# Edge sum of a graph layer: three of a group's seven edge lists get no blocks, their source rows are gathered edge by edge

## The chip, the cores and the metric

The kernel runs on one core of a Trainium2 chip. Its time is the device time of one execution in microseconds (us). TensorE is called PE in the profile (PEld is its weight loads), VectorE is DVE, ScalarE is ACT, GpSimd is POOL, and SyncE, which only issues transfers here, is SP.

## The reference, cut to what matters

```python
# x: 6250 x 256; src, dst: 200000 edges, sorted by dst; edge_weight: 200000
xn = _layernorm(x)
# _L0_gnn_ref: row = src, col = dst
gathered = edge_weight[:, None] * xn[dst]
gnn = segment_sum(gathered, src, 6250) + node_vec1
x = x + gnn + mix(xn)                 # linear attention, 4 heads
x = x + experts(_layernorm(x))        # 8 experts, the best 2 of each row
```

All is float32. The change lies in the second and third line: each edge adds its weight times row `dst` of `xn` to row `src` of the sum.

## The kernel before, in words

The 6250 rows are held as 49 tiles of 128 rows. `front` normalizes the rows and writes them to `xn_dram`; `edge_sum` makes the sum over the edges; `stragglers` looks for edges that found no place (none here); `route` and `experts` do the rest.

`edge_sum` has two jobs that run beside each other.

**Sorting.** Since the edges are sorted by `dst`, the edges of one dst tile lie in a row, and 49 steps `s` take one dst tile each. A step puts its edges into 49 lists by src tile, 128 slots a list (a list of one dst tile and one src tile is called a cell here). It needs `base` on PE (34 matmuls, L767), `hot_tiles`, `in_row`, `rank`, `slots` and `values` on VectorE (L992 to L1029) and `make_table` on PE (34 matmuls, L776). Its result, for each slot the src row in its tile, the dst row in its tile and the weight as three bfloat16 parts (FIELDS = 5), is copied by ScalarE into `table`. Eight steps run ahead of the sum (`schedule`, `sort`); the other 41 are spread over the sum's steps.

**Summing.** Seven dst tiles make a group `g` (7 groups), and for each group the kernel goes over the 49 src tiles: 343 steps `t`. Seven steps are a unit (`unit`, 49 units in all); the 42 units of the first six groups carry a sorting step each, the 7 units of the last group carry the normalization of the finished rows instead. A step `t` does, for the cells j = 0 to 6 of its group:

- VectorE, `hots` (L1063, L1067): one-hot matrices of the src and of the dst rows, slots on the partitions (`hots`, 2 x 7 x 128 elements a partition), and the src ones times the three parts of the weight (`hot_w`, 3 x 7 x 128).
- PE, `blocks` (L803): 7 x 3 bfloat16 matmuls, which sum over the slots and give for each cell a block, dst row by src row, of weights, in PSUM.
- ScalarE, `evacuate` (L910, L911): the seven blocks to `block_sb`.
- PE, `rows` (L811): 7 float32 matmuls, block times the 128 rows of the dst tile in `window`, summed in PSUM.
- VectorE, `add` (L1085): the sum to `acc`.

Each engine runs its instructions in the order in which `unit` writes them, and waits on semaphores. `blocks` of step t + 1 stand ahead of `rows` of step t; `hots` runs two steps ahead, `add` one behind. `cur` holds a unit's table values, each repeated 16 times by ScalarE (`take`, L904). GpSimd has no work in `edge_sum`. It issues transfers with row numbers from on-chip memory (indirect DMAs) only in `experts`: two gathers of 128 rows of 1032 bytes from `z_dram` (L1643) and two scattering additions into `sum_dram` (L1652) for each of 56 pieces.

## Time and profile before

| | us |
|---|---|
| median of 3 runs | 2680.07 |
| lowest, highest | 2675.88, 2681.29 |
| profiled execution | 2681.12 |
| its span | 2679.3 |

| stage (from, to in the span) | us | what runs |
|---|---|---|
| 0 to 415 | 415 | `front`, and eight sorting steps ahead |
| 415 to 1932 | 1517 | units 0 to 41: sum with sorting beside it |
| 1932 to 2168 | 236 | units 42 to 48: sum with normalization |
| 2168 to 2679 | 511 | `route`, `experts` |

The trace lists each instruction with its start and length; equal ones in a row are merged, and their length is that of the whole run. A float32 matmul has two records, so 7 matmuls of `rows` stand as x14. The waits that are printed name what an idle engine waited for; "issue" is time in which the engine waited for nothing that the profile shows.

### The profile page before, as it was taken

To read this page: it belongs to the slowest core of one execution; us is meant where nothing else is said; L and a number is where in the kernel's file an instruction comes from. 1 tells how busy PE (TensorE), PEld (TensorE's weight loads), DVE (VectorE), ACT (ScalarE), POOL (GpSimd) and SP (SyncE) were. 2 spreads that over 40 slices of the span, in tenths; PEclk is the share of its full clock that TensorE was granted. 3 is DMA by queue.
4 is the path that set the end of the run, shared out by engine and by line. 5 is a ranking of instruction groups with operands and counts; after the bars stand their busy time and mean duration, and the time that the engine had idled before them with its cause. 6 is when DMAs were issued, how large, how long until landed. Compare 5 with 4: busy or idle time off the path is not lost. (4 is left out here: it accounts for less than half of the span.)

```text
span 2679.3 us, 52157 instructions
## 1 busy us (share of the span) xinstructions
PE 2339.9 (87%) x19629; PEld 2059.4 (77%) x19630; DVE 2149.8 (80%) x2716; ACT 1382.2 (52%) x1876; POOL 451.9 (17%) x335
## 2 busy tenths in 40 slices
PE   4884679999999999999999999999999944999994
PEld 2553557888888888888888888888889944989983
DVE  5775769888988888898888899888888866766663
ACT  1223556556565555655555565555533324666662
POOL 2562000000000000000000000000000023888883
PEclk8997779999999999999999999999999967999997
DMA  6322230000000000000000000000011152444455
GB/s 159 85 81 80 69 97 15 0 0 2 14 0 0 15 1 0 0 15 1 0 0 16 1 0 0 15 0 0 1 42 56 56 168 45 75 76 76 75 78 129
DMA packets 124275, 103.46 MB, mean 39 GB/s; under 512 B 44684, under 2 KB 117879, under 8 KB 123892
## 3 DMA queue, kind: packets, MB, share of 16 engines
q1 hardware_dynamic: 95920, 71.42, 9.0%
q0 software_dynamic: 21504, 29.49, 7.2%
q10 hardware_dynamic: 6724, 0.83, 0.3%
q8 instruction: 83, 1.36, 0.2%
q14 instruction: 44, 0.36, 0.1%
HBM read 54.60 MB, written 53.51 MB: 40 GB/s over the span
## 5 line engine op out<-in xcount | busy, mean ns | idle before, releaser
L811 PE MATMUL bank<-window,block_sb 128*128 128x256 f32 x4802 | 1111.6, 383 | 0.0
L811 PEld LDWEIGHTS bank<-window,block_sb 128*128 128x128 f32 x4802 | 885.6, 190 | 106.2
L1067 DVE TENSOR_TENSOR hot_w<-hots,cur 128x2688 bf16<-128x2688 bf16 x343 | 534.4, 1558 | 11.9
L803 PE MATMUL bank<-hot_w,hots 128*128 128x128 bf16 x7203 | 458.8, 219 | 64.7 <-DVE hot_w L1067 62.6
L803 PEld LDWEIGHTS bank<-hot_w,hots 128*128 128x128 bf16 x7203 | 420.8, 98 | 117.7 <-DVE hot_w L1067 94.7
L910 ACT COPY block_sb<-bank 128x512 f32<-128x512 f32 x343 | 201.1, 586 | 568.9 <-PE bank L803 568.9
L1063 DVE TENSOR_TENSOR hots<-iota_j,cur 128x1792 bf16<-128x1792 bf16 x343 | 371.9, 1084 | 16.6 <-issue 11.5
L878 ACT COPY field_rep<-fields 128x3332 bf16 (+1 forms) x151 | 383.5, 2546 | 0.0
L1436 POOL MEMSET ones<- 128x128 bf16 x1 | 0.2, 204 | 1953.8 <-POOLq L1190 1953.8
L1085 DVE TENSOR_TENSOR acc<-acc,bank 128x256 f32 (+1 forms) x343 | 142.7, 416 | 166.2 <-PE bank L811 165.9
L1029 DVE TENSOR_TENSOR vals<-hot_t,field_rep 128x3332 bf16<-128x3332 bf16 x100 | 236.8, 2369 | 33.6 <-PE bank L776 33.6
L1652 POOL DMA_INDIRECT sum_dram<-acc,target x112 | 195.2, 1743 | 58.6 <-issue 31.7
L776 PE MATMUL bank<-vals,slot 128*128 128x245 bf16 x1700 | 192.5, 271 | 4.3 <-issue 4.3
L776 PEld LDWEIGHTS bank<-vals,slot 128*128 128x128 bf16 x1700 | 167.4, 99 | 27.7 <-issue 4.7
L904 ACT COPY cur<-table 128x2240 bf16 (+1 forms) x98 | 180.7, 1845 | 0.0
L911 ACT COPY block_sb<-bank 128x384 f32<-128x384 f32 x343 | 167.2, 487 | 0.0
L1745 PE MATMUL bank<-w,hh 128*128 x896 | 163.5, 282 | 1.8 <-DVE hl L1791 1.8
L1734 PE MATMUL bank<-zh,w1h 128*128 128x256 f32 x448 | 133.5, 298 | 24.6 <-DVE w1l L1785 23.1
L1745 PEld LDWEIGHTS bank<-w,hh 128*128 128x128 f32 x896 | 139.4, 191 | 2.2 <-issue 2.1
L1643 POOL DMA_INDIRECT acc<-z_dram,token x112 | 121.5, 1085 | 63.8 <-issue 30.8
L1734 PE MATMUL bank<-zl,w1h 128*128 128x256 f32 x448 | 128.4, 287 | 1.6 <-issue 1.6
L1734 PE MATMUL bank<-zh,w1l 128*128 128x256 f32 x448 | 128.3, 286 | 0.4 <-issue 0.3
(233 smaller groups left out, 2874.6 us busy)
## 6 DMA issues: line engine op xcount, KB each, us to landing
xn_dram<-xn SPq DMA_DIRECT2D x49, 128.0 KB, 1.7
xT_dram<-xT SPq DMA_DIRECT2D x49, 128.0 KB, 1.8
window<-xn_dram SPq DMA_DIRECT2D x7, 896.0 KB, 6.1
base_dram<-acc SPq DMA_DIRECT2D x7, 896.0 KB, 6.8
sum_dram<-acc SPq DMA_DIRECT2D x7, 896.0 KB, 4.2
z_dram<-vals SPq DMA_DIRECT2D x7, 896.0 KB, 7.0
out_dram<-sum_dram SPq DMA_DIRECT2D x1, 6250.0 KB, 21.9
w_all<-in_L_ffn_W_dram SPq DMA_DIRECT2D x8, 512.0 KB, 9.6
```

The costliest lines, as they stand in the source:

```text
L776: mm = pe.matmul(table_ps, slot[:, c, :], vals[:, c, :, :], start=(c == 0), stop=(c == CH - 1))
L803: mm = pe.matmul(block_ps(pp, j), hot[:, 1 + buf, j, :], hot_w[buf][:, part, j, :], start=(part == 0), stop=(part == 2))
L811: mm = pe.matmul(sum_ps[pp], block_sb[pp][:, j, :], window[par][:, j, :], start=(j == 0), stop=(j == GRP - 1))
L878: act.copy(field_rep[:, :, a:b, :], fields[:, a:b, bass.ds(s, 1), :].rearrange("p f a c -> p (a c) f").unsqueeze(3).broadcast_to([P, CH, b ...
L904: act.copy(cur[odd][:, a:b, :, :, :].rearrange("p i f g r -> p (i f g) r"), from_table[:, bass.ds(k * BU + a, b - a), :, :].rearrange("p i ...
L910: act.copy(block_sb[pp][:, 0:4, :].rearrange("p m c -> p (m c)"), banks[2 * pp][:, :])
L1029: dve.tensor_tensor(vals[:, :, a:b, :], hot_t[:, :, :].unsqueeze(2).broadcast_to([P, CH, b - a, NB]), field_rep[:, :, a:b, :], ALU.mult).t ...
L1063: dve.tensor_tensor(hot[:, 0:at + 1:at, :, :].rearrange("p f g (b r) -> p f g b r", r=REP), iota_j[:, :].rearrange("p (b r) -> p b r", r=R ...
L1067: dve.tensor_tensor(hot_w[i % 4][:, :, :, :].rearrange("p f g (b r) -> p f g b r", r=REP), hot[:, SRC, :, :].rearrange("p g (b r) -> p g b ...
L1652: pool.indirect_dma_start(out=sum_dram, out_offset=bass.IndirectOffsetOnAxis(ap=target[:, 2 * j + n:2 * j + n + 1], axis=0), in_=y[j % 2][ ...
L1734: mm = pe.matmul(hid_ps(i, c), ww[b][:, k * F + c * P:k * F + (c + 1) * P], zz[a][:, k, :], start=(m == 0), stop=(m == 5))
L1745: mm = pe.matmul(y_ps[i][:, n * D:(n + 1) * D], parts[a][:, c, n * P:(n + 1) * P], w, start=(m == 0), stop=(m == 3 * FC - 1))
```

## The change

Of the seven cells of a step, j = 0, 2, 4, 6 (DENSE = 4) are treated as before. The cells j = 1, 3, 5 (PICK = 3) get no block. For each of their 128 slots, the row `xn[dst]` is fetched by an indirect DMA from `xn_dram` to `picked` (128 slots x 256), and one float32 matmul sums over the slots with `pick_w`, the one-hot matrix of the src rows times the whole weight in float32. A slot without an edge has weight 0 and fetches the first row of the dst tile.

- **GpSimd** issues the gathers: 3 for each step, 1029 in all, in one line of code without a loop. Four sets of three buffers take turns (SETS = 4), so that a gather waits for `o_done` of the step three, four or seven back.
- **VectorE**: `hots` makes 11 one-hot matrices instead of 14 and `hot_w` 12 instead of 21; `picks` is new (3 x 128 elements, bfloat16 times float32 to float32). After three of each seven sorting steps `make_list` writes row numbers and float32 weights, three small instructions on 49 elements.
- **PE**: `blocks` has 12 matmuls instead of 21. `rows` still has 7 float32 matmuls of the same size, 4 from `block_sb` and `window`, and 3 from `pick_w` and `picked`, the latter behind a wait for the gathers.
- **ScalarE** copies 4 blocks instead of 7, repeats 23 table columns instead of 35, and repeats the float32 weights (`cur_w`).
- The windows hold 4 tiles instead of 7. The buffers that hold the transposed rows while the mix product is added ahead of the sum are other ones. Some semaphores are shared.

```diff
+        @block.gpsimd
+        def _(pool):
+            pool.wait_ge(mix_added, (GRP - 1) * BU)
+            for t in range(NG * NT):
+                g, b = divmod(t, NT)
+                i = t % BU
+                if b == 0:
+                    pool.wait_ge(listed, 2 * PICK * (g + 1))
+                used = t - SETS if i >= SETS else t - BU + SETS if i < BU - SETS else t - BU
+                if used >= 0:
+                    pool.wait_ge(o_done, used + 3)
+                for q in range(PICK):
+                    pool.indirect_dma_start(out=picked[:, i % SETS * PICK + q, :], out_offset=None, in_=xn_dram,
+                                            in_offset=bass.IndirectOffsetOnAxis(ap=place[g % 2][:, q, b:b + 1], axis=0)).then_inc(rows_in[i % SETS], 16)
...
-                for j in range(GRP):
+                for j in range(DENSE):
                     for part in range(3):
-                        mm = pe.matmul(block_ps(pp, j), hot[:, 1 + buf, j, :], hot_w[buf][:, part, j, :],
+                        mm = pe.matmul(block_ps(pp, j), hot[buf][:, PICK + DENSE + j, :], hot_w[buf][:, part, j, :],
                                        start=(part == 0), stop=(part == 2))
...
-                for j in range(GRP):
-                    mm = pe.matmul(sum_ps[pp], block_sb[pp][:, j, :], window[par][:, j, :], start=(j == 0), stop=(j == GRP - 1))
+                for j in range(DENSE):
+                    pe.matmul(sum_ps[pp], block_sb[pp][:, j, :], window[par][:, j, :], start=(j == 0), stop=False)
+                pe.wait_ge(pick_done, t + 2)
+                pe.wait_ge(rows_in[i % SETS], 16 * PICK * uses(i, u))
+                for q in range(PICK):
+                    mm = pe.matmul(sum_ps[pp], pick_w[i % SETS][:, q, :], picked[:, i % SETS * PICK + q, :], start=False, stop=(q == PICK - 1))
                 mm.then_inc(o_done, 1)
...
+            def make_list(s, n, q, par):
...
+                dve.wait_ge(unpacked, s + 1)
+                dve.tensor_tensor(place[par][:, bass.ds(q, 1), :].rearrange("p a b -> p (a b)"), raw[:, DST - 1, :],
+                                  first_row[:, bass.ds(s, 1)].broadcast_to([P, NB]), ALU.add)
+                dve.tensor_tensor(pair[:, :], raw[:, W - 1, :], raw[:, W, :], ALU.add).then_inc(listed, 1)
+                dve.wait_ge(listed, 2 * n + 1)
+                dve.tensor_tensor(weight[par][:, :, bass.ds(q, 1)].rearrange("p b a -> p (a b)"), pair[:, :], raw[:, W + 1, :], ALU.add).then_inc(listed, 1)
...
+            def picks(t, i, odd):
...
+                dve.wait_ge(hot_done, t + 1)
+                dve.tensor_tensor(pick_w[i % SETS][:, :, :].rearrange("p q (b r) -> p q b r", r=REP),
+                                  hot[i % SETS][:, 0:PICK, :].rearrange("p q (b r) -> p q b r", r=REP),
+                                  cur_w[odd][:, i, :, :].unsqueeze(2).broadcast_to([P, PICK, RUNS, REP]), ALU.mult).then_inc(pick_done, 1)
...
                 for i in range(BU):
+                    if i + 1 < BU:
+                        picks(t + i + 1, i + 1, odd)
+                    elif after:
+                        picks(t + BU, 0, 1 - odd)
```

How the instructions stand. On GpSimd before, between the last instruction of `front` (L292) and the unused part of `stragglers`, which begins with L1225 (`total` is a number of edges left over), `edge_sum` puts nothing:

```order
L292 CAST fields<-weight 128x238 [waits parts]
L176 UNCONDITIONAL_BRANCH
L1247 UNCONDITIONAL_BRANCH [waits barrier_Pool_Activation_PE_DVE_SP_gather]
L1225 TENSOR_LOAD total [waits total_done]
L1225 ISA x2
```

and in the changed kernel (`listed` counts finished lists, `o_done` finished steps):

```order
L291 CAST fields<-weight 128x238 [waits parts]
L175 UNCONDITIONAL_BRANCH
L763 UNCONDITIONAL_BRANCH [waits barrier_Pool_Activation_PE_DVE_SP_gather]
L775 DMA picked<-xn_dram,place 128x256 [waits listed,mix_added]
L775 DMA picked<-xn_dram,place 128x256 x11
L775 DMA picked<-xn_dram,place 128x256 [waits o_done]
L775 DMA picked<-xn_dram,place 128x256 x2
```

Twelve gathers stand ahead, the last two rows then repeat for each of the other 339 steps.

On VectorE, the first instructions of a unit in the loop before (`hots` and `hot_w` of the step two ahead, then parts of the sorting and `add`):

```order
L1063 TENSOR_TENSOR hots<-iota_j,cur 128x2x896
L1067 TENSOR_TENSOR hot_w<-hots,cur 128x2688
L1025 ISA
L1026 ISA
L1029 TENSOR_TENSOR vals<-hot_t,field_rep 128x34x98
```

and in the changed kernel:

```order
L1146 TENSOR_TENSOR pick_w<-hots,cur_w 128x384
L1135 TENSOR_TENSOR hots<-iota_j,cur 128x1408
L1138 REGISTER_ALU
L1139 TENSOR_TENSOR hot_w<-hots,cur 128x1536
L1086 ISA
L1087 ISA
L1090 TENSOR_TENSOR vals<-hot_t,field_rep 128x34x98
```

A `picks` stands ahead of each `hots`; the two that were there are shorter.

## Rows read from the trace of the kernel before

**Rows 1.** Page: busy tenths of POOL in 40 slices, and PE's granted clock.

```profile
POOL 2562000000000000000000000000000023888883
PEclk8997779999999999999999999999999967999997
```

**Rows 2.** Timeline, PE: start, length, line; a step, first bases of units, last group.

```profile
1004.06 1.33 PE L803 MATMUL bank<-hot_w,hots 128*128 128x128 bf16 x21
...
1005.24 3.24 PE L811 MATMUL bank<-window,block_sb 128*128 128x256 f32 x14
...
421.94 1.04 PE L767 MATMUL bank<-hot_t,before 128*128 128x49 bf16 x34
...
1899.73 1.04 PE L767 MATMUL bank<-hot_t,before 128*128 128x49 bf16 x34
...
2143.68 3.24 PE L811 MATMUL bank<-window,block_sb 128*128 128x256 f32 x14
...
2148.51 3.24 PE L811 MATMUL bank<-window,block_sb 128*128 128x256 f32 x14
```

**Rows 3.** Groups by line and shape, 500 to 1900: xcount, busy us, mean ns, idle.

```profile
L1067 DVE TENSOR_TENSOR hot_w<-hots,cur 128x2688 bf16<-128x2688 bf16 x272 | 423.8, 1558 | 9.4
L803 PE MATMUL bank<-hot_w,hots 128*128 128x128 bf16 x5691 | 362.7, 219 | 57.8 <-DVE hot_w L1067 55.7 <-issue 2.1
...
L1063 DVE TENSOR_TENSOR hots<-iota_j,cur 128x1792 bf16<-128x1792 bf16 x271 | 293.7, 1084 | 11.1 <-issue 11.1
...
L1029 DVE TENSOR_TENSOR vals<-hot_t,field_rep 128x4998 bf16<-128x4998 bf16 x39 | 109.6, 2811 | 0.0
L1085 DVE TENSOR_TENSOR acc<-acc,bank 128x256 f32 x237 | 98.5, 416 | 104.0 <-PE bank L811 104.0
L1020 DVE TENSOR_TENSOR slot<-iota_j,rank_rep 128x4352 bf16<-128x4352 bf16 x39 | 94.3, 2419 | 0.0
L1029 DVE TENSOR_TENSOR vals<-hot_t,field_rep 128x3332 bf16<-128x3332 bf16 x39 | 75.1, 1926 | 0.0
...
L1005 DVE TENSOR_TENSOR earlier<-hot_t,base_sb 128x1666 bf16<-128x1666 bf16 x39 | 40.7, 1043 | 0.0
...
L1010 DVE TENSOR_TENSOR earlier<-earlier 128x816 bf16<-128x816 bf16 x39 | 22.8, 585 | 1.4
```

**Rows 4.** One unit: busy us of PE, PEld, DVE, ACT, POOL, then clock, DMA.

```profile
1000.00:1036.00 36.00, 34.44 (x313) 30.43 (x311) 32.48 (x32) 20.99 (x25) 0.00 (x0) 1.00 0.00 0
```

**Rows 5.** The gathers of `experts`: ns min/median/max of the line, then timeline rows.

```profile
L1643 POOL DMA_INDIRECT acc<-z_dram,token x112: 944/986/2019, 2245.9 to 2614.3; - x112
...
2249.98 0.95 POOL L1643 DMA_INDIRECT acc<-z_dram,token  x1 [0.30 <-issue]
...
2252.73 1.11 PE L1724 MATMUL bank<-ident,acc 128*128 128x128 f32 x4 [1.39 <-DMA acc<-z_dram,token]
...
2256.24 0.95 POOL L1643 DMA_INDIRECT acc<-z_dram,token  x1 [0.30 <-issue]
```

**Rows 6.** Indirect DMAs beside VectorE in `experts`: timeline, and the summary of L1652.

```profile
2301.34 1.23 DVE L1785 TENSOR_TENSOR w1l<-w_all,w1h 128x1024 fp32r<-128x1024 f32 x1
2301.45 2.02 POOL L1643 DMA_INDIRECT acc<-z_dram,token  x1 [0.30 <-issue]
2302.49 0.68 DVE L1791 TENSOR_TENSOR hl<-acc,hh 128x512 fp32r<-128x512 f32 x1
...
L1652 POOL DMA_INDIRECT sum_dram<-acc,target x112: 1547/1620/2624, 2275.5 to 2653.5; - x112
...
2368.78 1.23 DVE L1785 TENSOR_TENSOR w1l<-w_all,w1h 128x1024 fp32r<-128x1024 f32 x1
2368.95 2.52 POOL L1652 DMA_INDIRECT sum_dram<-acc,target  x1 [0.30 <-issue]
2369.93 1.28 DVE L1791 TENSOR_TENSOR hl<-acc,hh 128x512 fp32r<-128x512 f32 x2
```

**Rows 7.** A stretch of `experts`, columns as in rows 4.

```profile
2370.00:2400.00 30.00, 26.83 (x221) 25.89 (x220) 19.84 (x39) 18.53 (x34) 24.82 (x18) 1.00 0.49 74
```

More of the change, by code:

```diff
@@ L590, in edge_sum @@
     AHEAD = GRP + 1
+    DENSE, PICK = (GRP + 1) // 2, GRP // 2
+    ROWS = FIELDS * DENSE + PICK
+    HOTS = PICK + 2 * DENSE
+    SETS = 4
+    assert 4 * DENSE * P * 4 == 2 * DENSE * D * 4 and DENSE * P == 512 and SETS * PICK >= BU and 2 * DENSE >= BU
     with ExitStack() as ctx:
@@ L648, in turn_ps @@
         def turn_ps(n):
-            return banks[0 if n > LATE and n % 2 == 0 else 7][:, 0:D]
+            return banks[2 if n > LATE and n % 2 == 0 else 7][:, 0:D]
         xT_in = [sem(f"xT_in{i}") for i in range(2)]; mixed = sem("mixed"); mix_added = sem("mix_added")
@@ L660, in edge_sum @@
         hot_done = sem("hot_done"); w_done = sem("w_done"); a_done = sem("a_done"); a_copied = sem("a_copied")
-        o_done = sem("o_done"); o_added = sem("o_added"); placed = sem("placed")
+        o_done = sem("o_done"); o_added = sem("o_added")
+        listed = sem("listed"); pick_done = sem("pick_done"); rows_in = [sem(f"rows_in{i}") for i in range(SETS)]
         block = ctx.enter_context(nc.Block())
@@ L705, in load_xT @@
                 of = xT_dram[at, :].rearrange("(t p) c -> p t c", p=P)
-                if c % 2:
-                    sp.dma_start(window[1][:, :, :], of).then_inc(xT_in[1], 16)
-                else:
-                    for k in range(2):
-                        sp.dma_start(block_sb[k][:, :, :], of[:, :, k * P:(k + 1) * P]).then_inc(xT_in[0], 16)
+                to = picked[:, 0:BU, :] if c % 2 else stage[:, 0:BU * D].rearrange("p (t d) -> p t d", d=D)
+                sp.dma_start(to, of).then_inc(xT_in[c % 2], 16)
             sp.dma_start(M, M_dram.rearrange("p (k d) -> p k d", k=2)).then_inc(small_in, 16)
@@ L817, in begin, with unit @@
                 blocks(0, 0, 0)
-            def unit(g, k, odd, par, turn, more, after):
+            def unit(g, k, odd, par, turn, more, after, q):
                 t = g * NT + k * BU
@@ L924, in begin, with unit @@
                 act.wait_ge(unpacked, GRP)
-                take(0, 0, table[0], 0, 0)
-                take(0, 0, table[0], 0, 1)
+                act.wait_ge(listed, 2 * PICK)
+                take(0, 0, 0, 0, 0)
+                take(0, 0, 0, 0, 1)
                 unpack(AHEAD - 1, 0, 1)
                 evacuate(0, 0)
-            def unit(g, k, odd, par, turn, more, after):
+            def unit(g, k, odd, par, turn, more, after, q):
                 u = g * GRP + k
@@ L1073, in begin, with unit @@
                 hots(0, 0, 0, None)
+                picks(0, 0, 0)
                 hots(1, 1, 0, None)
                 dve.wait_ge(saved, 16 * GRP)
-            def unit(g, k, odd, par, turn, more, after):
+            def unit(g, k, odd, par, turn, more, after, q):
                 u = g * GRP + k
```

134 lines of the change are left out of this document (83 added, 51 removed).

## The prediction

> **What bounds the kernel now.** I read three views in turn. First the page's slices: GpSimd does nothing from slice 5 to slice 31, which is the edge sum, and PE's clock is full there [rows 1]. So the engine that gets the new work is free, and nothing has to be paid for a slow clock. Then the busy times of one unit: PE 34.4 of 36.0 us, VectorE 32.5, ScalarE 21.0 [rows 4]. PE is the bound, VectorE is close behind it. Last the timeline of PE: a step is 1.18 us of `blocks` (from 1004.06 to 1005.24) and then the seven matmuls of `rows` [rows 2]. PE waits for `hot_w` for 57.8 us in the 39 units of the stretch, 1.5 us a unit [rows 3]: where the sorting instructions stand between two `hots`, VectorE sets the pace. The length of a unit is read from the first `base` of unit 0 and of unit 41: (1899.73 - 421.94) / 41 = 36.04 us [rows 2]. A step of the last group takes 2148.51 - 2143.68 = 4.83 us [rows 2].
>
> **What the change takes away.** PE: 9 of 21 matmuls of `blocks`, at 1.18 / 21 = 0.056 us each, 0.51 us a step, 3.5 us a unit. The number and size of the float32 matmuls stay, so they cost the same. ScalarE has 40% of its time free already, and its saving and its copies of `cur_w` lie beside other work: nothing. VectorE: `hots` and `hot_w` differ by 1558 - 1084 = 474 ns for 896 elements [rows 3], 0.53 ns an element over a start of 0.14 us. With 1408 and 1536 elements they take 0.88 and 0.95 us instead of 1.08 and 1.56. The new `picks` has float32 in it; the nearest rows are `w1l` with 1.23 us for 1024 float32 elements and `hl` with 0.68 for 512 [rows 6], 1.07 ns an element over 0.13: 0.54 us for 384. By bfloat16's rate it would be 0.34; I take 0.54, since its type is that of those rows. VectorE saves 2.64 - 2.37 = 0.27 us a step, 1.9 a unit, less 0.3 for the lists (nine instructions of 49 elements in seven units, each near the 0.14 us start, and their waits): 1.6.
>
> **If nothing else came in**, a unit would shrink by 3.5 us if PE's work set it alone, by 1.6 if VectorE's did. I take 2.5, a unit of 33.5 us. This is not my forecast, because of the next part.
>
> **What the change adds on GpSimd.** A unit has 21 gathers. The trace has 112 gathers of the same kind, one row more or less of 1 KB each: 0.95 us when nothing else runs, 0.99 in the median, and 0.30 us to the next one, which is there also with nothing to wait for [rows 5]. So 1.29 us each, 27.1 us a unit: beside 33.5 us it would be hidden.
>
> But the longest gather took 2.02 us. It started at 2301.45, when `w1l` on VectorE had 1.12 us to run; it took 1.03 more than the median, and `hl` began without a gap at the end of `w1l` [rows 6]. The scattering DMAs show the same: the median is 1.62; one that started when `w1l` had 1.06 us to run took 2.52, 0.90 more [rows 6]. Both `w1l` and `hl` read two operands from SBUF. Sorted by what was on VectorE at their start, the gathers and scatters that began during such an instruction are longer by what was left of it less some 0.1 us, also where the next one followed at once, and those that began beside instructions with an operand in PSUM are not longer. A gather has to read its 128 row numbers from SBUF, and I take it that this read waits for the running instruction to end, and then gets in.
>
> In the edge sum nearly all of VectorE's work is of this kind. For a gather that starts at any moment, the mean wait is the sum of the squared lengths over twice the period. Lengths a unit: seven times 0.88, 0.95 and 0.54, squared 7 x 1.97 = 13.8; 2.81, 2.42 and 1.93, squared 17.5; five more between 0.59 and 1.04, taken as 0.81 [rows 3], squared 3.3. That is 34.6 / (2 x 36) = 0.48 us, less 0.1 x 0.77 (the share of time in which one runs: 16.6 + 7.2 + 4.1 = 27.9 of 36): 0.40. The step's own order makes this uncertain: three gathers in a row meet the same few instructions again and again. I take 0.43. A gather then costs 1.29 + 0.43 = 1.72 us, and 21 of them 36.1 us. **GpSimd would become the bound at almost exactly the old 36.04.**
>
> The Trainium skill's page "SBUF — State Buffer", section "Who interferes with whom", says that a VectorE instruction with two SBUF inputs contends with a GpSimd instruction that reads SBUF. By that sentence the trace agrees: 2.02 against 0.99 us. The same section has two more statements that would lead elsewhere, and both are weighed with the rivals.
>
> **Can the gathers' own latency show?** From the end of the fourth gather (2250.93) to PE's first use of it (2252.73) it is 1.8 us [rows 5]. A gather of step t may start when step t - 3 is done, so two steps of some 5 us lie between: hidden. If GpSimd is the bound, it never waits for `o_done` either, since PE ends a step about 1.8 + 3 x 0.44 = 3.1 us after its last gather. The first twelve gathers, 12 x 1.72 = 21 us, may start with the sixth list and the 42nd of 49 mix additions, a sorting step and more ahead of the sum: they cost nothing, or a few us at worst. PE would be idle 5 us in 36; in `experts` it is busy 26.8 of 30 and keeps clock 1.00 [rows 7], so I put nothing for the clock.
>
> **The last group.** PE would need 4.83 - 0.51 = 4.32 us a step. GpSimd: VectorE's three long instructions give 1.97 / (2 x 4.4) = 0.22, less 0.05, and a gather costs 1.29 + 0.17 = 1.46, three 4.38 us. I take 4.43, as the two nearly meet: 49 x 0.40 = 20 us saved.
>
> **Sum**, on the profiled execution's 2681: 42 units x (36.1 - 36.04) = +3; last group -20; three lists in the eight sorting steps ahead, +2: 2666. The execution was 1 us above the median: 2665.
>
> **Rivals.**
>
> 1. *The gathers are not held up* (the waits in `experts` have another cause, or the bfloat16 instructions leave gaps). Then the units take 33.5: 42 x 2.5 = 105, last group 49 x 0.51 = 25; 2681 - 130 + 2 = 2553, say 2552. For it: GpSimd has 27.1 us of work only. Against it: the extra time follows the rest of the running instruction. The Trainium skill, same page and section, notes that a `tensor_tensor` was not seen to stall a DMA issued by GpSimd; by that rule this case holds. 15%.
>
> 2. *A gather misses turns.* In `experts` VectorE runs at most three such instructions in a row; in the edge sum they come without end, and a waiting gather may lose to the next one. Each lost turn costs the mean length of one, 27.9 / 29 = 0.96 us. If one gather in ten loses one, a unit grows by 2.0 us and the kernel by 84, with 3 to 14 more in the last group: 2665 + 95 = 2760; one in three gives +340, 3000. It decides as soon as GpSimd's unit is over 36.5, which is one turn lost in fifty gathers. An unlucky phase of the three gathers (a mean wait of 0.55 instead of 0.43) has the same sign: +106. Against it: none of the longest scatters, which met `w1l` with `hl` right behind, missed a turn. 17%.
>
> 3. *The gather holds VectorE.* Each row number read keeps VectorE from its second operand for h us. VectorE would need 32.5 - 1.6 = 30.9 + 21 h, and beats GpSimd's 36.1 from h = 0.25. The Trainium skill, same page and section, says that whichever starts first has the shared ports for its whole instruction; by that, h would be 0.95, and a unit 51 us: 2681 + 42 x 15 + 49 x 1.2, about 3350. Against it in the rows: `hl` started at 2302.49, inside a gather that ran to 2303.47, with its usual 0.68 us [rows 6]. 5%.
>
> 4. *As forecast*, GpSimd is the bound with waits of one rest each: a mean wait between 0.30 and 0.55 us gives units from 33.5 (where VectorE and PE take over) to 38.6 us. 63%.
>
> **How the numbers follow.** In case 4 the time is 2665 with some 45 us to both sides, as 0.05 us on a gather is 44 us on the kernel in the loop alone; 0.2% (5 us, about what a measurement of this kernel can tell from no change) is a narrow band in that. Below 2675 lies 0.57 of it, within the band 0.10, above 0.33. Faster: 0.15 + 0.63 x 0.57 = 0.51. Same: 0.06. Slower: 0.22 + 0.21 = 0.43. The likeliest case's own range is 2605 to 2725. The range of 8 in 10 must take in most of rival 1 and the mild end of rival 2: from 2550 to 2790, with some 8% below and 12% above.
>
> **What would show it.** GpSimd busy over 70% of slices 6 to 31, 0.30 us between gathers and hardly a wait for `o_done`; gathers of 0.95 us at the shortest and 1.4 in the mean, none over 0.99 + 2.8; PE idle ahead of the `picked` matmuls and released there by the DMA; a unit of 36 us, and `blocks` of 0.67 us. `picks` at 0.54 and `hots` and `hot_w` at 0.88 and 0.95 us check VectorE. If PE waits for `hot_w` as before and GpSimd waits for `o_done`, rival 1 holds. If gathers of 3 us and more are common, rival 2. If the same VectorE instruction takes longer or starts later beside a gather, rival 3. The forecast is wrong above all if the mean gather is off by more than 0.1 us.

## The result

The changed kernel took **2602.1 us** (median, 2600.2 to 2611.5) beside 2680.6 us of the kernel before (2675.9 to 2681.3) on the same chip: ratio 0.972, 95% interval 0.969 to 0.974. The forecast was 2665. So it is faster, as forecast, but by 78.5 us where 15 were expected. In a later set of runs, on another chip, the same changed kernel took 2550.5 us beside 2673.9 (ratio 0.954, interval 0.953 to 0.955). The second half of this text is about what tells the two apart; it finds where the 50 us lie, not their last cause.

First the page of the changed kernel on the first chip: busy times, then the slices that answer to [rows 1], and two DMA queues.

```profile
span 2600.7 us, 47621 instructions
...
PE 2205.2 (85%) x16542; PEld 1907.9 (73%) x16543; DVE 2047.2 (79%) x3123; ACT 1197.2 (46%) x1603; POOL 1682.1 (65%) x1364
...
POOL 2563005777777777767777777777765633888883
PEclk9997778999999999999999999999998958999997
...
q0 software_dynamic: 70896, 164.43, 25.2%
...
q8 instruction: 71, 1.16, 0.2%
```

GpSimd is busy 7 tenths of the edge sum, and the granted clock is at nine tenths or more from the eighth slice to the end of the loop. Now the groups by line from 500 to 1900, which answer to [rows 3] (count, busy us, mean ns, idle before and what ended it):

```profile
L775 POOL DMA_INDIRECT picked<-xn_dram,place x867 | 1040.9, 1201 | 359.5 <-issue 245.2 <-PE bank L851 98.4 <-remote 15.9
L851 PE MATMUL bank<-picked,pick_w 128*128 128x256 f32 x1728 | 423.5, 381 | 0.0
...
L1139 DVE TENSOR_TENSOR hot_w<-hots,cur 128x1536 bf16<-128x1536 bf16 x290 | 277.8, 958 | 10.1
L1135 DVE TENSOR_TENSOR hots<-iota_j,cur 128x1408 bf16<-128x1408 bf16 x289 | 255.9, 886 | 0.1
L839 PE MATMUL bank<-hot_w,hots 128*128 128x128 bf16 x3468 | 243.1, 219 | 87.4 <-DVE hot_w L1139 63.1 <-issue 22.6 <-ACT stage L964 1.7
...
L1146 DVE TENSOR_TENSOR pick_w<-hots,cur_w 128x384 f32<-128x384 bf16 x290 | 160.1, 552 | 9.8 <-issue 9.8
```

A gather takes 1.20 us in the mean, and the next one starts 0.30 us later: 1.50 us, 31.5 us a unit. PE never waits for gathered rows (line 851, idle 0.0). GpSimd waits for PE (98.4 us in this stretch, whose last 90 us are the last group; 89.8 of them lie before 1800), and PE for `hot_w` (63.1 us), as before (55.7). So **GpSimd is not the bound of the loop**.

Where the time went is read from three instants: the first `base` of unit 0, the start of the last matmul of the last `base` (0.9 us behind that unit's first), and the last sum added. The summaries of these lines, of the kernel before, then of the changed one:

```profile
L767 PE MATMUL bank<-hot_t,before x1700: 183/185/223, 256.5 to 1900.6; 128*128 128x49 bf16 x189
L1085 DVE TENSOR_TENSOR acc<-acc,bank x343: 412/415/422, 424.6 to 2165.1; 128x256 f32 x126, 128x256 f32<-128x256 f32 x46
```

```profile
L803 PE MATMUL bank<-hot_t,before x34: 183/185/187, 421.6 to 422.5; 128*128 128x49 bf16 x34
...
L803 PE MATMUL bank<-hot_t,before x1700: 183/185/223, 255.1 to 1811.6; 128*128 128x49 bf16 x189
L1165 DVE TENSOR_TENSOR acc<-acc,bank x343: 412/415/423, 424.1 to 2086.8; 128x256 f32 x126, 128x256 f32<-128x256 f32 x46
```

A unit of the loop: (1811.6 - 0.9 - 421.6) / 41 = 33.88 us, where it was 36.04. That is 41 x 2.16 = 88.6 us. The **last stretch**, from the last `base` to the last sum (the rest of unit 41 and the seven units of the last group), went from 1900.6 to 2165.1 before = 264.5, and from 1811.6 to 2086.8 now = 275.2: 10.7 us longer, where 20 less were forecast. The rest of the kernel stayed within 0.7 us. The sum is 2679.3 - 2600.7 = 78.6.

### The profile page after: what moved, and what is told of

It reads as the page before. It is cut to its first block and busy times, and to the rows that moved or that the text cites. A ratio compares the mean times of both kernels' runs of the same rounds, so it can differ in the third digit from the quotient of the medians.

```text
span 2600.7 us, 47621 instructions
## 1 busy us (share of the span) xinstructions
PE 2205.2 (85%) x16542; PEld 1907.9 (73%) x16543; DVE 2047.2 (79%) x3123; ACT 1197.2 (46%) x1603; POOL 1682.1 (65%) x1364
## 5 line engine op out<-in xcount | busy, mean ns | idle before, releaser
L775 POOL DMA_INDIRECT picked<-xn_dram,place x1029 | 1230.1, 1195 | 615.1 <-issue 287.3
L964 ACT COPY stage<-bank 128x512 f32<-128x512 f32 x343 | 208.9, 609 | 650.6 <-remote 459.8
L851 PE MATMUL bank<-picked,pick_w 128*128 128x256 f32 x2058 | 505.8, 382 | 0.0
L851 PEld LDWEIGHTS bank<-picked,pick_w 128*128 128x128 f32 x2058 | 396.2, 193 | 56.0 <-issue 0.2
L847 PE MATMUL bank<-window,stage 128*128 128x256 f32 x1568 | 393.8, 395 | 7.9 <-issue 5.9
L1139 DVE TENSOR_TENSOR hot_w<-hots,cur 128x1536 bf16<-128x1536 bf16 x343 | 328.6, 958 | 11.9
L847 PEld LDWEIGHTS bank<-window,stage 128*128 128x128 f32 x1568 | 289.8, 195 | 43.9 <-issue 8.1
L1135 DVE TENSOR_TENSOR hots<-iota_j,cur 128x1408 bf16<-128x1408 bf16 x343 | 303.6, 885 | 0.1
L847 PE MATMUL bank<-stage 128*128 128x256 f32 x1176 | 290.9, 391 | 9.8 <-issue 7.9
L847 PEld LDWEIGHTS bank<-stage 128*128 128x128 f32 x1176 | 214.2, 192 | 36.0 <-issue 8.9
L1146 DVE TENSOR_TENSOR pick_w<-hots,cur_w 128x384 f32<-128x384 bf16 x343 | 189.3, 552 | 11.9 <-issue 10.3
```

Source lines behind the costliest of these rows:

```text
L775: pool.indirect_dma_start(out=picked[:, i % SETS * PICK + q, :], out_offset=None, in_=xn_dram, in_offset=bass.IndirectOffsetOnAxis(ap=plac ...
L847: pe.matmul(sum_ps[pp], block_sb[pp][:, j, :], window[par][:, j, :], start=(j == 0), stop=False)
L851: mm = pe.matmul(sum_ps[pp], pick_w[i % SETS][:, q, :], picked[:, i % SETS * PICK + q, :], start=False, stop=(q == PICK - 1))
L1135: dve.tensor_tensor(to[:, :, :].rearrange("p f (b r) -> p f b r", r=REP), iota_j[:, :].rearrange("p (b r) -> p b r", r=REP).unsqueeze(1).b ...
L1139: dve.tensor_tensor(hot_w[i % SETS][:, :, :, :].rearrange("p f g (b r) -> p f g b r", r=REP), to[:, PICK:PICK + DENSE, :].rearrange("p g ( ...
```

## Experiment 1: is the wait of a gather what the forecast took it for?

The mechanism was forecast as: a gather that starts while a VectorE instruction with two SBUF inputs runs waits for its end. Here is the timeline of the changed kernel (start, length, engine, line):

```profile
1008.38 0.88 DVE L1135 TENSOR_TENSOR hots<-iota_j,cur 128x1408 bf16<-128x1408 bf16 x1
1008.53 1.55 POOL L775 DMA_INDIRECT picked<-xn_dram,place  x1 [0.30 <-issue]
1009.29 0.96 DVE L1139 TENSOR_TENSOR hot_w<-hots,cur 128x1536 bf16<-128x1536 bf16 x1
1010.17 0.41 DVE L1165 TENSOR_TENSOR acc<-acc,bank 128x256 f32 x1
...
1010.38 0.94 POOL L775 DMA_INDIRECT picked<-xn_dram,place  x1 [0.30 <-issue]
1010.50 2.81 DVE L1090 TENSOR_TENSOR vals<-hot_t,field_rep 128x4998 bf16<-128x4998 bf16 x1
...
1011.63 2.49 POOL L775 DMA_INDIRECT picked<-xn_dram,place  x1 [0.30 <-issue]
...
1014.42 0.97 POOL L775 DMA_INDIRECT picked<-xn_dram,place  x1 [0.30 <-issue]
```

The gather at 1011.63 started when `vals` had 1.68 us to run, and took 2.49 - 0.95 = 1.54 us more than one that meets nothing. The one at 1008.53 met 0.73 us of `hots`: 0.60 more. The one at 1010.38 started during `acc`, which reads PSUM, and took 0.94. I sorted all 889 gathers from 420 to 1860 us by the VectorE instruction that ran at their start (worked out from rows like these):

```
instruction running      gathers   its rest, us   extra over 0.95, us
hots      (SBUF, SBUF)     263        0.24            0.12
acc       (SBUF, PSUM)     263                        0.00
vals      (SBUF, SBUF)      81        1.69            1.55
slot      (SBUF, SBUF)      39        1.04            0.91
rank      (one input)       38                        0.00
hot_w     (SBUF, SBUF)      33        0.63            0.50
none                        50                        0.00
```

(The other 122 met shorter or rarer instructions: `earlier` 66, `picks` 33, `same` 18, five others.) The extra is the rest less 0.12 us, within 0.02, and nothing where the rest is shorter than that; of all 889 one differs, a gather that began 2 ns after a `picks` and took 0.95. No gather in the loop missed a turn: the mechanism holds. Nor is VectorE held up: of 268 `hot_w` between 500 and 1800 us, 242 began while a gather ran, and they took 958 ns, as the 26 others did and as all do without gathers. But the mean extra is 0.25 us, not 0.43. With the lengths of this trace, a start at any moment would give 0.43 (the sum of (length - 0.12) squared over two, for the 1161 such instructions from 500 to 1800, over 1300 us). The starts are not spread evenly: a gather gets in when an instruction ends, and the next one starts 0.95 + 0.30 = 1.25 us later, which is often near the end of `picks` and `hots` (0.47 + 0.91 us from start to start) or during `add`. More than half of the 889 fall on `hots` near its end and on `add` (`acc` in the table). The waits set the phase of what follows.

To see a gather's price where GpSimd sets the pace, a fourth gather was added to each step:

```diff
+                if t:
+                    pool.wait_ge(spare_in, 16 * t)
+                pool.indirect_dma_start(out=spare[:, :], out_offset=None, in_=xn_dram.rearrange("n (a c) -> (n a) c", c=P),
+                                        in_offset=bass.IndirectOffsetOnAxis(ap=place[g % 2][:, 0, b:b + 1], axis=0)).then_inc(spare_in, 16)
```

> Added: a fourth gather a step, of 128 rows of 512 B, into a spare buffer that nobody reads; GpSimd must become the bound with 28 gathers a unit. Theory (a gather costs 1.25 us and the rest of the two-SBUF-input instruction of VectorE that runs at its start, and this rest is 0.25 on average because starts follow the ends of VectorE's instructions): 28 x 1.50 = 42.0 us a unit, total 2601 + 49 x 8.1 = about 3000, range 2930 to 3060. Rival A (starts fall anywhere: mean wait 0.43, 1.72 each): 48.2 a unit, total about 3290. Rival B (the short rows make it cheaper, or more gathers hold VectorE up): unit under 40, or VectorE's instructions longer than 885 ns (hots).

It took 3021.6 us, ratio 1.126 (1.123 to 1.128), a unit 42.6 us. Groups by line from 500 to 2150:

```profile
L777 POOL DMA_INDIRECT picked<-xn_dram,place x808 | 939.9, 1163 | 327.9 <-issue 232.5 <-remote 86.0 <-PE bank L857 9.4
...
L781 POOL DMA_INDIRECT spare_rows<-xn_dram,place x269 | 300.5, 1117 | 81.9 <-issue 81.9
```

The mean is (939.9 + 300.5) / 1077 = 1.15, with the gap 1.45 us; 28 of them 40.7. The other 2 us of the unit are one wait (`remote` and `PE bank` in the first row, 95 us in 38 units): the first gather of a unit's third step waits for `o_done` of the step three back, and by the trace's semaphore records `o_done` changes up to 8.9 us after that step's last matmul ended. At 1013.55, for instance, the matmul ended at 1004.37 and `o_done` changed at 1013.29. So the 42.0 that I expected was met partly by luck. The forecast's 1.72 would have given 48.2 and 3290 us. 1.45 to 1.50 us is the price. The late semaphore comes back below.

## Experiment 2: what do the gathers cost, and where?

All gathers and PE's wait for them were left out (lines 766 to 776 and the wait in `rows`), then those of the last seven units only, then the stores of the sums:

```diff
-            for t in range(NG * NT):
+            for t in range((NG - 1) * NT):
...
-                pe.wait_ge(rows_in[i % SETS], 16 * PICK * uses(i, u))
+                if more:
+                    pe.wait_ge(rows_in[i % SETS], 16 * PICK * uses(i, u))
```

> Left out: the gathers on GpSimd and TensorE's wait for their rows; the three picked matmuls of a step read rows of zeros that are written once, so the output is wrong. Theory: GpSimd is not the bound of the loop (21 x (1.20 + 0.30) = 31.6 of 33.9 us a unit), TensorE and VectorE are, so the loop gains 0 to 0.4 us a unit; the seven units after it, 246 us with the gathers where 49 steps of 4.43 were expected, are long because the gathers' traffic stands beside the stores there, and fall to about 220: 2560 to 2575 us. Rival A (GpSimd is the bound of the loop after all): unit 33.9 to 33.0 or less, total under 2545. Rival B (the last units are long for a reason that is not the gathers: the stores, or the straight-line program of that part): they stay at 240 to 246, total 2590 to 2601.

> Left out: the gathers of the last seven units only (147 of 1029) and TensorE's wait for them; it reads the rows that happen to stand in the buffers, so the output is wrong. Theory (gathers beside the stores make the last units long): the loop stays at 33.9 us a unit, the last seven fall from 246 to about 220 us, total 2572 to 2580. Rival B (the stores or the straight-line program alone): 2596 to 2601.

> Left out: the seven stores of the finished sums in the last seven units; in their place the rows of before are copied from DRAM to DRAM in the middle of the loop (group 4), so the output is wrong. Theory (gathers beside stores): the last seven units fall from 246 to some 225 to 235 us (the stores of z are left), and the stretch of the loop beside the copies shows units of over 35 us: 2580 to 2595 in all. Rival A (the gathers alone delay the straight-line part): the last units stay at 246 us, total 2600 or more. Rival B (the stores alone): the last units at about 220.

These runs shared one chip: without gathers 2553.6 us (unit 33.61, last stretch 238.8); without those of the last units 2556.5 (33.68, 240.4); without the sum stores 2598.5 (33.95, 269.3). So the gathers cost the loop next to nothing, and the last stretch 29 us (269.3 against 240.4), or 35 by the 275.2 of the first result. The first two totals lie below my ranges (from 2560 and 2572 on): I had put the last stretch's loss at 26 us. The forecast had PE at 4.32 us a step of the last group; without gathers the steps take 4.31 in the mean. The stores are at most a small part. The rival in which GpSimd bounds the loop has fallen, and so has the one that blames the stores alone.

Five more runs took the gathers of the last units apart. The first two shared a chip; in one, all gathers fetched 128 B a row in place of 1 KB, in the other the last units' gathers went to a buffer that nobody reads:

```diff
-                    pool.indirect_dma_start(out=picked[:, i % SETS * PICK + q, :], out_offset=None, in_=xn_dram,
+                    pool.indirect_dma_start(out=picked[:, i % SETS * PICK + q, 0:32], out_offset=None, in_=xn_dram.rearrange("n (a c) -> (n a) c", c=32),
```

```diff
+                    to, told = (spare[:, n % 2 * PICK + q, :], spare_in[n % 2]) if n >= 0 else (picked[:, i % SETS * PICK + q, :], rows_in[i % SETS])
```

> Changed: each of the 1029 gathers fetches 128 rows of 128 B in place of 128 rows of 1 KB (the rest of the picked rows is zeros, so the output is wrong); the number of gathers and of their packets' rows stays. The last seven units take 35 us more with gathers than without. Theory (the gathers' bytes on the DMA engines delay something there): most of it comes back, 2565 to 2575 us in all. Rival A (the gathers as such, by their number, do it): 2592 to 2602. A gather of short rows is expected to cost GpSimd the same 0.95 us and 0.30 behind it, since that time would be the writing of 128 descriptors; if it is the transfer, it falls.

> Changed in the last seven units only: the gathers are issued as in the change, with the same waits for TensorE, but into a buffer that nobody reads, and TensorE takes rows of an earlier group without a wait, so the output is wrong. Theory (the gathers get in the way of something else, such as the fetch of instructions): the last units stay long, total 2592 to 2602 us. Rival (TensorE waits for rows that land late): they fall to the length without gathers, total 2555 to 2568.

2600.1 and 2601.1 us, last stretches of 266 and 273: neither the bytes nor a wait for the rows matter. A gather of short rows keeps GpSimd as long (938 ns at the shortest, 964 in the median).

The others, on a third chip, were one gather a step in the last units, three copies of 128x256 within SBUF on GpSimd, and three direct DMAs of 128 KB from SyncE's queue:

```diff
-                for q in range(PICK):
+                for q in range(PICK if n < 0 else 1):
```

```diff
+                    if n >= 0:
+                        pool.tensor_copy(spare[:, 2 + q, :], spare[:, 0, :]).then_inc(spare_in[0], 1)
+                        continue
```

```diff
+                for q in range(PICK):
+                    sp.dma_start(spare[:, n % 2 * PICK + q, :], xn_dram[(3 * n + q) % NT * P:((3 * n + q) % NT + 1) * P, :]).then_inc(spare_in[n % 2], 16)
```

> As the run in which nobody waits for the last seven units' gathers (they go to a buffer that nobody reads), but with one gather a step there in place of three. With three the stretch from the last tile count of the loop to the last sum takes 273 us, with none 240. Theory (each fetch of code waits behind the gathers that are under way, so the loss goes with their number): a third of the loss, 250 to 254 us, total 2572 to 2580. Rival A (any gather beside the written-out code costs all of it): over 265 us, total over 2590. Rival B (the loss starts only where GpSimd issues without a pause): under 244 us, total 2555 to 2565.

> In the last seven units GpSimd makes three copies of 128x256 f32 a step within SBUF, with the same waits, in place of the three gathers; TensorE takes rows of an earlier group, so the output is wrong. Theory (the gathers' requests to the DMA engines delay the fetch of code): no request, no loss, the last stretch 240 to 244 us, total 2555 to 2565. Rival (GpSimd at work, or its turns with VectorE at SBUF, delays the others): 255 us or more, total over 2572, or VectorE's instructions longer than without.

> In the last seven units SyncE issues three direct DMAs of 128 rows of 1 KB a step (fixed rows, into a buffer that nobody reads), paced like the gathers, in place of them; the stores stay; TensorE takes rows of an earlier group, so the output is wrong. Theory in the form that any traffic of that kind delays the fetch: the last stretch 260 to 275 us, total 2585 to 2605. Rival (it is the gathers' own way, descriptors that GpSimd writes, that delays it): 240 to 246 us, total 2556 to 2568.

2559.5, 2562.9 and 2563.0 us, with last stretches of 239.7, 245.3 and 238.8: no loss in the first and third, at most 6 us in the one with copies. That chip does show the loss: a run on it that keeps all gathers (PE's code written out, below) has a last stretch of 268.8. One gather a step costs nothing, so the loss does not go with the number from the first on, as my theory had it; it sets in between one and three gathers a step. Two were never run on a chip that shows the loss. The copies took 0.39 us at the shortest, so GpSimd was less busy in that run than with gathers; it tells less than I had wanted.

## What the loss looks like

In the last units of the run in which nobody waits for the gathers, by 5 us (busy us of PE, PEld, DVE, ACT, POOL, then clock, DMA share, GB/s):

```profile
1875.00:1880.00 5.00, 5.00 (x41) 4.48 (x39) 1.80 (x5) 0.58 (x1) 3.78 (x5) 1.00 0.38 105
1880.00:1885.00 5.00, 3.27 (x24) 2.47 (x22) 4.73 (x13) 0.00 (x0) 3.91 (x4) 1.00 0.91 283
1885.00:1890.00 5.00, 2.54 (x8) 2.10 (x9) 0.80 (x1) 2.08 (x3) 3.96 (x4) 0.84 0.32 91
1890.00:1895.00 5.00, 2.44 (x7) 1.62 (x6) 0.95 (x4) 0.00 (x0) 3.78 (x5) 0.82 0.32 98
1895.00:1900.00 5.00, 1.75 (x9) 1.21 (x10) 3.02 (x5) 0.00 (x0) 2.27 (x3) 0.52 0.35 100
1900.00:1905.00 5.00, 4.64 (x14) 3.61 (x14) 3.48 (x6) 1.35 (x3) 3.52 (x3) 0.50 0.19 56
```

From 1880 to 1900 PE is busy for 10 of 20 us; the granted clock falls between 1885 and 1900 and is at 0.50, the level of 1.2 GHz, from 1900 to 1905, where PE works at half speed. It falls below 0.9 in four places of this stretch (from 1885, 1950, 1995 and 2065 on), of which this is the longest. The whole last stretch of the changed kernel, on the first chip and then on the later one where it is short (same columns):

```profile
1812.00:2087.00 275.00, 250.63 (x1688) 218.63 (x1686) 199.36 (x364) 76.83 (x130) 178.63 (x160) 0.94 0.40 114
```

```profile
1798.00:2042.00 244.00, 235.09 (x1690) 209.80 (x1687) 196.57 (x364) 77.77 (x131) 182.61 (x160) 0.99 0.45 128
```

The same PE work takes 15.5 us more at the lower clock (250.63 against 235.09), and PE is idle for 15.5 us more (24.4 against 8.9): half of the 31 us is the clock that PE's pauses cost. In the places of the loss engines start late (again the run in which nobody waits):

```profile
1886.83 0.58 ACT L973 COPY stage<-bank 128x512 f32<-128x512 f32 x1 [10.60 <-remote]
...
1893.97 0.42 DVE L1174 TENSOR_TENSOR acc<-acc,bank 128x256 f32<-128x256 f32 x1 [8.18 <-remote]
...
1895.53 0.69 PE L796 MATMUL bank<-ident,vals 128*128 128x128 f32 x2 [3.09 <-issue]
...
1898.91 0.26 PE L847 MATMUL bank<-hot_w,hots 128*128 128x128 bf16 x1 [1.86 <-issue]
```

ScalarE's copy starts 2.4 us after the last matmul of the blocks that it copies (ended at 1884.44). "remote" means that the semaphore changed so long after the instruction that changes it that the view names none. The trace also has the times at which semaphores change, which no view prints: this one changed at 1886.80, and the copy started 0.03 us later. For `acc` at 1893.97 the last matmul ended at 1892.44 and `o_done` changed at 1893.95. So ScalarE and VectorE start at once when told; **it is PE's semaphore that changes late**. Over the loop of the changed kernel on the first chip (500 to 1800 us), 232 of the 557 recorded changes of PE's semaphores come over 0.5 us after the matmul that makes them, the latest 4.7 us; the 1551 recorded ones of ScalarE's and VectorE's semaphores all come within 0.01 us. The same kernel on the later chip: none late, PE's neither. (All these are worked out from the records, one change for one instruction.)

PE itself waits 3.09 and 1.86 us for nothing shown ("issue"), once in the middle of a row of twelve matmuls. The last group is written out without a loop, so its code is executed once. That led to the theory that the code's fetch is delayed by the gathers.

## Experiment 3: written-out code

Six of each group's seven units, so far a loop of three turns, were written out, on all engines; the same without gathers:

```diff
-                with eng.Fori(0, GRP // 2) as q:
+                for q in range(GRP // 2):
```

> Changed: six of a group's seven units, two to a loop of three turns so far, are written out one behind the other on every engine; a loop is left over pairs of groups, whose code is 14 units long. Nothing that is computed or issued changes. Theory (code that an engine executes for the first time must be fetched, and the gathers' transfers delay the fetch; the last seven units, written out, lose 5 us a unit by it): the 42 units of the loop now lose about as much, 34 to some 37 to 39 us a unit, total 2730 to 2810 us. Rival (written-out code is not what makes the last units long): 2592 to 2605 us.

> The units in a row, and no gathers (as in the run without gathers, rows of zeros are read, the output is wrong). Theory (only gathers together with written-out code cost time): as without gathers in loops, 2550 to 2565 us. Rival (written-out code costs by itself): over 2600 us.

2644.1 us with gathers and 2544.2 without, on the chip where the two runs with loops gave 2600.1 and 2601.1. So written-out code costs nothing by itself (the run without gathers in loops, 2553.6, was on another chip) and 43 us more with gathers there: the direction is the theory's, but the size is a third to a fifth of the 130 to 210 us that it gave. The unit of the loop is 34.65 us there, 33.35 without gathers. Then one engine at a time, by a flag that `schedule` takes (its lines are left out here):

```diff
-            schedule(dve, sort, begin, unit, finish, ended)
+            schedule(dve, sort, begin, unit, finish, ended, True)
```

> Only TensorE's program has the units of the loop written out one behind the other; the other engines' programs loop as in the change. With all engines written out the time was 2644, with none 2601 us. Theory (it is TensorE's code whose fetch is late, it has some 60 instructions a step): 2625 to 2645. Rival (the other engines' code, or GpSimd's): 2595 to 2610.

> Only ScalarE's program has the loop's units written out. With all engines written out the time is 2644, with TensorE alone 2581, with none 2602 us. If it is the fetch of ScalarE's code that the gathers delay: 2635 to 2665. If it is VectorE's: 2595 to 2608.

> Only VectorE's program has the loop's units written out. If it is the fetch of VectorE's code that the gathers delay: 2635 to 2665. If it is ScalarE's: 2595 to 2608. If both of this pair stay under 2610, it takes several engines fetching at once.

PE's alone took 2581.3 us, on the third chip, where the change itself was not run; its last stretch is 268.8 and its loop's unit 33.66. That is against the theory, although its code fetches rose (in the page: `q8 instruction: 123` where the change has 71). ScalarE's took 2548.4 and VectorE's 2540.7: below everything that any kernel with all its gathers had taken, against both theories at once. Two more runs were made beside them:

> As the run with one gather a step in the last seven units that nobody waits for, with two. The last stretch takes 240 us with none and with one, 273 with three. Theory (the loss starts where GpSimd issues gathers without a pause: two take 2.5 to 3 of 4.3 us): 240 to 246 us, total 2557 to 2568. Rival (it goes with the number, past some number): 252 to 262 us, total 2570 to 2585.

> Left out: both kinds of stores in the last seven units; rows of before are copied from DRAM to DRAM in the middle of the loop in their place, so the output is wrong. All gathers stay and are waited for. Theory (it takes the stores and the gathers together): the last stretch 240 to 248 us. Rival (the gathers alone do it): 262 to 275 us. The total also holds what the copies cost in the loop, some 5 to 10 us; without sum stores it was 2598.

2547.4 and 2562.8 us (last stretches 241.4 and 239.5). Both stretches are what my theories gave, but they test neither: all four runs had been on a chip that no earlier run had used, and none of them shows a late start. So the last two runs, on yet another chip, put the change itself beside one of them:

> The changed kernel as it is, timed in turns with the one with VectorE's units in a row. If the loss beside the gathers (the last stretch 275 in place of 240 us, ScalarE's late starts in the loop) depends on the chip: this kernel is within 25 us of the other one here, both near 2540 to 2560 us without the late starts, or both near or above 2590 with them. If it depends on the code's layout: this one takes 2595 to 2610 and the other one 2536 to 2550.

> VectorE's program alone with the loop's units written out, as in the run of 2541 us. If the loss depends on the chip: 10 to 20 us under the change where neither shows late starts; where both show them, near it or above, since more code is fetched. If on the code's layout: 2536 to 2550, whatever the change does.

**The change itself took 2550.5 us**, ratio 0.954 (0.953 to 0.955), and VectorE's units in a row 2537.6, ratio 0.949 (0.948 to 0.950). So the code is not it: the same kernel is 50 us apart. By the two profiles (58 us apart) 31 us lie in the last stretch, 14 behind the last sum, 9 in the loop and 4 ahead of it. It was the chip, or something that changed with the time at which the runs were made, since both chips without the loss were used last. What tells the two kinds apart is in the waits from 500 to 1800 us (in total, times, longest). First the changed kernel on the first chip, then the same code here:

```profile
ACT stage L964 <- remote: 384.4, 97, 6.6
...
ACT stage L964 <- PE bank L839: 127.3, 54, 6.2
...
PE bank L839 <- DVE hot_w L1139: 56.4, 56, 1.4
```

```profile
ACT stage L964 <- PE bank L839: 489.9, 196, 3.9
POOL picked L775 <- issue: 232.5, 763, 0.3
...
PE bank L839 <- DVE hot_w L1139: 96.3, 81, 1.8
```

ScalarE's waits that end with a late semaphore (97 times some 4 us here, part of which ScalarE would wait anyhow) are in every profile with gathers up to here (59 to 103 of them; the first result and the chips of the first three sets of runs), and in none from the two later chips. They cost the loop little: a unit is 33.88 us with them and 33.65 without. Without gathers they are absent on the first kind of chip too.

The kernel before takes 2672 to 2674 us on the later chips where the others gave 2680 to 2683. It has no gathers in the edge sum, but it has indirect DMAs in `experts`, and there its own profile shows the same: from 2200 to 2500 us, 23 of the 130 recorded changes of PE's semaphores come over 0.5 us late, and none of 576 in its loop. What follows the last sum takes 2679.3 - 2165.1 = 514.2 us in it, 510 to 514 in every run of the first kind, and 500 to 507 on the later chips, where no change is late there either. So these 8 us are of the same kind, and the sign stood in the trace of before.

One more thing goes with it. In those stretches the records of semaphore changes have holes: in the loop of the changed kernel on the first chip 512 of 2063 of ScalarE's and VectorE's are missing, in `experts` of the kernel before 162 of 670, and in the same stretches of the changed kernel on the later chip one of 2822. Whether the recording of the trace takes part in the loss, or only suffers from the same cause, no run here can tell.

The last group on the later chip:

```profile
L803 PE MATMUL bank<-hot_t,before x1700: 183/185/223, 253.9 to 1797.8; 128*128 128x49 bf16 x189
L1165 DVE TENSOR_TENSOR acc<-acc,bank x343: 411/415/423, 420.4 to 2042.1; 128x256 f32 x126, 128x256 f32<-128x256 f32 x46
```

and busy times of it there, and without gathers on the first kind of chip:

```profile
1866.00:2040.00 174.00, 170.82 (x1256) 154.34 (x1255) 138.14 (x275) 51.28 (x99) 131.76 (x115) 1.00 0.50 141
```

```profile
1866.00:2030.00 164.00, 164.00 (x1215) 148.40 (x1214) 132.42 (x268) 49.99 (x96) 0.00 (x0) 1.00 0.17 57
```

The last stretch is 2042.1 - 1797.8 = 244.3 us: 20.2 less than before, and 5.5 more than without gathers (PE is idle 3.2 us of the first window and not at all in the second).

**What is settled and what is not.** Shown: in the first four sets of runs, a nearly gapless stream of GpSimd's indirect DMAs goes with late changes of PE's semaphores, by which the other engines start late; it took some 30 us in the last stretch by the runs that shared a chip (2556.5 against 2598.5 us in all), and 100 us with all code written out (2544.2 against 2644.1). One gather a step or direct DMAs of the same size don't do it, and copies at most a fifth; the bytes and the wait for rows are not it. The fetch of code does not make the semaphores late, as far as the trace has its packets. In the changed kernel on the first chip, from 505 to 619 us, the DMA queues and the longest wait are:

```profile
q0 software_dynamic: 3456, 9.44, 28.0%
```

```profile
ACT stage L964 <- remote: 41.7, 9, 6.6
```

No queue of kind "instruction" is among them (the nearest such packets start at 494.4 and 619.5), and yet ScalarE's copies were told late as often as elsewhere. Where code is fetched, its packets take no longer: 0.85 us in the mean from 500 to 1800 there, 0.88 on the later chip, 0.91 without gathers.

Open: what delays PE's semaphores, and why written-out code of all engines makes the loss larger, when PE's alone does not; ScalarE's and VectorE's alone were only run where the effect is absent. What differs between the chips, or between the times of the runs, I can't say either.

## The prediction, point by point

- **PE and VectorE's savings: right.** `hots` 0.886, `hot_w` 0.958, `picks` 0.552 us against 0.88, 0.95 and 0.54. "If nothing else came in, a unit would be 33.5 us": without gathers it is 33.61. (Of the 57.8 us that I read as PE's wait for `hot_w`, 55.7 are that wait [rows 3].)
- **The mechanism of the wait: right.** A gather waits for the rest of the running two-input instruction, and VectorE is not held up (the causes of rivals 1, 2 and 3 all fall). The Trainium skill's page "SBUF — State Buffer", section "Who interferes with whom", notes that a `tensor_tensor` was not seen to stall a DMA that GpSimd issues, and that the first to start has the ports for its whole instruction. The first does not carry over to these gathers, which read their row numbers from SBUF: 81 of them waited 1.55 us for `vals`. The second agrees where VectorE was first, and disagrees where the gather was: `vals` began at 1010.50 inside a gather that ran from 1010.38 and took its usual 2.81 us, and the 242 `hot_w` that began inside a gather took their 0.96.
- **The price of a gather: this is the term that failed.** It stood at 1.72 us: 0.99 + 0.30 + 0.43. It measured 1.50: 0.95 + 0.30 + 0.25 (1.45 with four gathers a step). I took the median 0.986 of [rows 5] as the bare cost; that median already held some waiting, and I then added the waiting again. And I took the mean wait for a start at any moment, though I had written that three gathers meet the same few instructions; the waits bring the starts near the ends. 21 x 0.22 = 4.6 us a unit turned a bound of 36.1 into 31.5, under the 33.7 of PE and VectorE. "GpSimd would become the bound" is wrong for the loop by this, and so are its signs (PE held up by the gathered rows, hardly a wait for `o_done`); the +3 us of the sum became -88.6.
- **The forecast's own warning** was that it fails if the mean gather is off by more than 0.1 us. It was off by 0.22 (1.20 against 1.42). My likeliest case held 0.30 to 0.55 for the wait; the true 0.25 lay just outside, where rival 1's figures begin.
- **Rival 1**, 2552 us at 15%, had the wrong mechanism (gathers not held up) and, by luck, the right time: 2550.5 on the later chip. It should have been "the gathers are held up, but not enough to matter", with a larger chance: the bound has a kink there, and below a price of 33.5 / 21 = 1.60 us GpSimd costs nothing.
- **The last group: right where the late starts are absent** (-20.2 against -20), wrong by 31 us on the first chip (+10.7). The late semaphores were a term that I put at nothing. The trace of before has no gathers in the edge sum [rows 1], but it does have late changes of PE's semaphores beside the indirect DMAs of `experts`, from which I read the gathers' price; I had not looked for them.
- **PE's clock: right in the loop.** In the last group on the first chip it fell to 0.50 behind PE's pauses, which I had not in the sum: 15.5 of the 31 us.
- **Latency hidden: right.** PE waits 0.0 us for `picked` in the loop.

**A faster version.** VectorE's units written out beat both kernels where they were timed in turns, 2537.6 against 2550.5 and 2673.9 us; a unit is 33.39 in place of 33.65. VectorE's 13 waits of "issue" ahead of `picks` (10.3 us), where its loop turns, are 2 (7.4 us) then; that explains 3 of the 11 us that the loop gained, and the rest is not shown. On the chips with late starts it wasn't run, and writing out all engines lost 43 us on one of them.

## To carry to other kernels

Where an engine's new work comes near the bound, the result hangs on a few hundredths of a microsecond of price; write the forecast with the kink, and ask at which price the new engine begins to count. Mean waits by the sum of squares are for starts at any moment; an engine that waits for another's instruction to end starts its next work in step with it. When an engine starts late, look whether it was told late. And compare only runs that shared a chip: ScalarE's and VectorE's written-out code seemed to bring 50 us until the unchanged kernel was run beside it.

## What the runs showed of the hardware

An indirect gather of 128 rows costs GpSimd 0.94 us and 0.30 us to the next, for rows of 128 B as for 1 KB. It adds the rest, less 0.12 us, of a VectorE instruction with two SBUF inputs that runs at its start, and nothing beside one that reads PSUM or has one input (889 gathers, one exception); VectorE's instructions take as long beside it. The time of the kernel with 1029 gathers differs by 2% between the first runs and those on another chip (2602 and 2550 us) where that of the kernel before differs by 0.3% (2681 and 2674). In the longer ones PE's semaphores change up to 4.7 us late in the loop and up to 8 in the last group (8.9 with four gathers a step), ScalarE's and VectorE's never; why is open.
